# A Mamba block between two feed-forward layers: output blocks copied out of PSUM by ScalarE and added up by GpSimd, and rings of seven for x and the gate

## The reference

```
proj = x @ in_proj                      # gate (4096), x (4096), B and C (128 each), dt (64 heads)
x, B, C = silu(conv4(x, B, C) + bias)   # causal, 4 taps, per channel
dt = softplus(dt + dt_bias);  cum = cumsum(dt * A) in chunks
scores = (C B^T) * exp(cum_i - cum_j) * dt_j        # masked, in a chunk
y = scores @ x + exp(cum) * (C @ state) + D * x     # state: scan over chunks
h = y * silu(gate)
out = (h * rsqrt(mean(h^2)) * norm_w) @ out_proj    # 4096 -> 256
```

## Time and profile before

| | |
|---|---|
| median of 3 runs | 1473.42 us |
| the profiled execution | 1473.38 us, its span 1471.7 us |
| TensorE (PE) busy | 1333.7 us, 91% |
| VectorE (DVE) busy | 1191.9 us, 81% |
| ScalarE (ACT) busy | 1007.0 us, 68% |
| GpSimd (POOL) busy | 820.3 us, 56% |

### The profile page before, as it was taken

The page is one execution under the profiler, slowest core; times in us unless marked ns, Lnnn a source line. Parts: engine busy times, 40 slices in busy tenths (PEclk is TensorE's granted clock), DMA queues, the critical chain, the costliest instruction groups (busy, mean ns, idle before and its releaser), DMA issues. The chain is left out here.

```text
span 1471.7 us, 27111 instructions
## 1 busy us (share of the span) xinstructions
PE 1333.7 (91%) x8896; PEld 1134.4 (77%) x8896; DVE 1191.9 (81%) x2643; ACT 1007.0 (68%) x2067; POOL 820.3 (56%) x896
## 2 busy tenths in 40 slices
PE   5889887767999999999999999999999999986998
PEld 4778766556888878888888888888888888864887
DVE  5753433676999999999999999999999999986433
ACT  1114433667889988888988898888899888861332
POOL 1004211004678777878877787797787878681000
PEclk9999998988999999999999999999999999996999
DMA  6221000222444444453444444444444444334000
GB/s 128 66 86 36 15 6 10 58 65 73 125 111 98 126 117 109 119 115 98 119 128 108 117 105 116 116 122 117 112 104 120 123 110 116 94 80 185 15 14 29
DMA packets 102085, 136.43 MB, mean 93 GB/s; under 512 B 27744, under 2 KB 49856, under 8 KB 101824
## 3 DMA queue, kind: packets, MB, share of 16 engines
q1 hardware_dynamic: 99840, 132.67, 34.4%
q10 hardware_dynamic: 2112, 2.10, 0.4%
HBM read 124.76 MB, written 9.96 MB: 92 GB/s over the span
## 5 line engine op out<-in xcount | busy, mean ns | idle before, releaser
L845 ACT ACTIVATE M<-cum_row,cum_table 128x128 f32<-128x128 f32 x1024 | 312.1, 390 | 0.0
L1272 DVE SCALAR_TENSOR_TENSOR xs<-psum,conv_w_sb,xs 128x509 f32<-128x509 f32 (+2 forms) x384 | 283.2, 738 | 0.4
L985 POOL TENSOR_TENSOR hid_lo<-hid,hid_hi 128x512 fp32r<-128x512 f32 x128 | 196.2, 1533 | 67.3 <-PE psum L40 61.5
L1060 POOL TENSOR_TENSOR hid<-hid,sg 128x512 f32<-128x512 f32 x128 | 165.5, 1293 | 94.0 <-DVE hid L1340 93.9
L1049 POOL TENSOR_TENSOR squares<-squares,sq 128x512 f32<-128x512 f32 x124 | 160.0, 1290 | 75.3 <-ACT sq L822 75.3
L1299 DVE TENSOR_TENSOR M<-M,CB 128x1024 f32<-128x1024 f32 x128 | 183.5, 1434 | 0.0
L1655 PE MATMUL psum<-M,xdt 128*64 128x128 f32 x2048 | 140.1, 278 | 24.3 <-DVE psum L1331 24.2
L827 ACT ACTIVATE sg<-psum 128x512 f32<-128x512 f32 x128 | 75.1, 587 | 104.5 <-PE psum L40 96.9
L1655 PEld LDWEIGHTS psum<-M,xdt 128*64 128x64 f32 x2048 | 110.1, 136 | 47.2 <-DVE M L1299 27.4
L1632 PE MATMUL psum<-xend,B_tok 128*128 128x128 f32 x1024 | 140.1, 281 | 2.5 <-DVE carry L1323 2.4
L853 ACT ACTIVATE M<-M 128x1024 f32<-128x1024 f32 x128 | 134.5, 1051 | 0.5
(11 more groups left out here) (210 smaller groups left out, 3422.0 us busy)
## 6 DMA issues: line engine op xcount, KB each, us to landing
cum_row<-cum_scratch SPq DMA_DIRECT2D x256, 256.0 KB, 4.4
e_row<-e_scratch SPq DMA_DIRECT2D x256, 128.0 KB, 3.4
xw_raw<-L_attn_in_proj_w_dram SPq DMA_DIRECT2D x32, 128.0 KB, 3.3
wo_raw<-L_attn_out_proj_w_dram SPq DMA_DIRECT2D x32, 128.0 KB, 3.0
gw_raw<-L_attn_in_proj_w_dram SPq DMA_DIRECT2D x16, 256.0 KB, 4.5
x_res<-_attn_hidden_states_dram ACTq DMA_DIRECT2D x4, 512.0 KB, 9.4
x_scratch<-x_res SPq DMA_DIRECT2D x4, 512.0 KB, 2.6
x_res<-x_scratch SPq DMA_DIRECT2D x1, 2048.0 KB, 8.0
```

The source lines that it names most:

```text
L845: last = nc.scalar.activation(M[:, v % 3, h, c * CH:(c + 1) * CH], cum_row[:, v % 2, h, c * CH:(c + 1) * CH], ACT.Relu, bias=scalar_of(CUM ...
L985: nc.gpsimd.tensor_tensor(hid_lo[:], hid[:, v % 2, :], hid_hi[:, v % 2, :].bitcast(F32), ALU.subtract).then_inc(hid_lo_done, 1)
L1060: nc.gpsimd.tensor_tensor(hid[:, v % 2, :], hid[:, v % 2, :], sg[:, v % 8, :], ALU.mult).then_inc(hid_done, 1)
L1272: nc.vector.scalar_tensor_tensor(xs[:, v % 8, shift:], psum[:, X_BANK + v % 2, 0:TT - shift], tap_of(v, step), xs[:, v % 8, shift:], ALU.m ...
```

## The change

VectorE's `add_out` goes. In its place ScalarE copies both banks to a new tile `part` (two halves, one buffer) with `take_out`, right behind `square(s)` of the next phase round; GpSimd adds the halves to `mixed` with `add_part`, one in the third and one in the fourth round of the next group of four, behind `split_hid`. In the first group of pairs ScalarE copies straight into `mixed`. `out_proj` now waits for the copies (`out_taken`), and `take_out` waits until `part` has been added up (`mixed_done`). The rings `xs` and `sg` lose one place each, so that `evac_g(v)` waits for `gate(v-7)` and `evac_x(v)` for `skip_path(v-7)`. Second definitions of two helpers, and an unused one, are deleted too; they change no instruction.

```
-    xs = sb("xs", [P, 8, TT], F32)
-    sg = sb("sg", [P, 8, TT], F32)
+    xs = sb("xs", [P, 7, TT], F32)
+    sg = sb("sg", [P, 7, TT], F32)
...
+    part = sb("part", [P, KT, TT], F32)
...
             def evac_g(v):
                 act.wait_ge(g_proj, nth(v))
-                act.wait_ge(hid_done, nth(v - 8))
+                act.wait_ge(hid_done, nth(v - 7))
...
             def evac_x(v):
                 act.wait_ge(x_proj, nth(v))
-                act.wait_ge(v_done, nth(v - 8))
+                act.wait_ge(v_done, nth(v - 7))
...
+            def take_out(v):
+                t = at_slot(v)[1]
+                act.wait_ge(out_done, nth(v))
+                if v == GP - 1:
+                    act.wait_ge(cum_out, 16 * 2 * NT)
+                if v >= SLOTS:
+                    act.wait_ge(mixed_done, KT * ((v - SLOTS) // GP))
+                for m in range(KT):
+                    to = mixed[:, m, tile(t)] if v < SLOTS else part[:, m, :]
+                    nc.scalar.activation(to, psum[:, OUT_BANK + m, :], ACT.Copy).then_inc(out_taken, 1)
...
             for s in range(-8, ALL):
                 if alive(s):
                     square(s)
+                if s > 0 and s % GP == 0:
+                    take_out(s - 1)
                 phase = s % GP == 0 and alive(s + 4)
...
+            take_out(ALL - 1)
...
+            def add_part(v, m):
+                t = at_slot(v)[1]
+                pool.wait_ge(out_taken, KT * (v // GP) + m + 1)
+                nc.gpsimd.tensor_tensor(mixed[:, m, tile(t)], mixed[:, m, tile(t)], part[:, m, :],
+                                        ALU.add).then_inc(mixed_done, 1)
...
                     gate(s + 1)
                     split_hid(s + 1)
                 g, u = divmod(s, SLOTS)
+                if s % GP in (2, 3) and SLOTS <= s - s % GP - 1:
+                    add_part(s - s % GP - 1, s % GP - 2)
...
+            for m in range(KT):
+                add_part(ALL - 1, m)
...
-                if s >= 0 and s % GP == GP - 1:
-                    add_out(s)
...
                 if j == 0:
-                    pe.wait_ge(mixed_done, KT * (v // GP))
+                    pe.wait_ge(out_taken, KT * (v // GP))
```

More of the change, by code:

```diff
@@ L470, in macaron @@
     halo_in, halo_step, halo_done = sem("halo_in"), sem("halo_step"), sem("halo_done")
-    folded = sem("folded")
+    folded, out_taken = sem("folded"), sem("out_taken")
     wo_hi_done, wo_lo_done, hid_hi_done, hid_lo_done = [sem(n) for n in ("wo_hi_done", "wo_lo_done", "hid_hi_done", "hid_lo_done")]
@@ L1009, in split_wo @@
                 split_wo_lo(p)
[L1011 to L1034, removed]
-                                        ALU.subtract).then_inc(wo_lo_done, 1)
-            def hid_to_lo(v):
-                pool.wait_ge(hid_hi_done, nth(v))
-                pool.wait_ge(sq_done, nth(v))
-                nc.gpsimd.tensor_tensor(hid_lo[:, v % 2, :], hid[:, v % 2, :], hid_hi[:, v % 2, :].bitcast(F32),
-                                        ALU.subtract).then_inc(hid_lo_done, 1)
             def add_squares(v):
@@ L1339, in skip_path @@
                 p = pair_of(v)
-                nc.vector.scalar_tensor_tensor(hid[:, v % 2, :], xs[:, v % 8, :], d_sb[:, p:p + 1], bank(Y_BANK),
+                nc.vector.scalar_tensor_tensor(hid[:, v % 2, :], xs[:, v % 7, :], d_sb[:, p:p + 1], bank(Y_BANK),
                                                ALU.mult, ALU.add).then_inc(v_done, 1)
-            def add_out(v):
-                j, t = at_slot(v)
-                dve.wait_ge(out_done, nth(v))
-                if v == GP - 1:
-                    dve.wait_ge(cum_out, 16 * 2 * NT)
-                for m in range(KT):
-                    if v < SLOTS:
-                        nc.vector.tensor_copy(mixed[:, m, tile(t)], psum[:, OUT_BANK + m, :]).then_inc(mixed_done, 1)
-                    else:
-                        nc.vector.tensor_tensor(mixed[:, m, tile(t)], psum[:, OUT_BANK + m, :], mixed[:, m, tile(t)],
-                                                ALU.add).then_inc(mixed_done, 1)
             dve.wait_ge(lut_in, 16)
@@ L1620, in turn_x @@
                 for c in range(CPT):
-                    last = nc.tensor.transpose(psum[:, XT_BANK, c * P:(c + 1) * P], xs[:, v % 8, c * CH:(c + 1) * CH], ident[:])
+                    last = nc.tensor.transpose(psum[:, XT_BANK, c * P:(c + 1) * P], xs[:, v % 7, c * CH:(c + 1) * CH], ident[:])
                 last.then_inc(x_turned, 1)
```

16 lines of the change are left out of this document (8 added, 8 removed).

## The result

The changed kernel takes 1606.99 us (median of 4 runs, 1606.28 to 1611.78) against 1473.57 (4 runs on the same chip): ratio 1.0913, 95% interval 1.0885 to 1.094, or +133.4 us. The forecast was 1583, a loss of 110. The profiled span is 1604.6 us against 1471.7; TensorE is busy 1379.7 us of it (86%, before 91%) at a mean granted clock of 0.938 (0.969).

What follows compares the result with a forecast made beforehand. It took the path from ScalarE's phase round through `e_row` and `scale_off` to TensorE's `diag` to have no slack. 1473.4 + 88.6 (copies, wait, end) + 21 (clock) = 1583 us; range 1495 to 1640, the forecast's own 1540 to 1630.

Steps and rivals of the forecast that it cites:

- the wait for `part`: From round 24 on, ScalarE's copies wait 2.2 us for GpSimd's second add; with copies, 82.6 us over 25 stretches.
- the loop: Copies, ScalarE's phase work, `e_row`, `diag`, two TensorE rounds, `hid_lo`, add, next copies: 33.3 to 35.2 us per four rounds.
- VectorE's adds go: VectorE loses 32 pairs of 1.28 us, 41 us in all; nothing gained on the path, since `e_row` ends there too.
- copies on ScalarE: Two PSUM copies, 1.20 us, ahead of each phase round's table load; 4 us in rounds 4 to 20, without waiting.
- adds on GpSimd: 72 us of adds have room beside GpSimd's 161 of 200; later `hid_lo` costs 0 to 8 us, taken as 0.
- ring of seven, under the wait: `evac_g` 1.1 us later behind its round's gate, hidden by the copies' wait (up to 2.2 us): 0; uncovered 27 us.
- What would show it: ScalarE idle 2 us before copies, some 25 waits for `e_row`, TensorE idle 3 us, stretches 33 to 37 us.
- two rounds of TensorE, `hid_lo`: Way from `diag(71)` to `hid_lo` of 72, which starts when `out_proj` ends: 13.20 us from s = 68.
- as the one from u = 4 ... so I take 3.4 for it too: Stretch from u = 8, with the weight load behind `e_row`: +3.4 us, as from s = 68.
- rival 4: VectorE's adds were the true limit, `e_row` early enough: 35 us less, 2 more at the end, 1440 us; chance 0.05.
- The clock: TensorE's idle time halves its clock for one block, 1.27 us, in two of three of 25 stretches: 21 us.
- Rival 2: Every TensorE stall halves the clock for two blocks' worth, 64 us: 1626 us; chance 0.09.

Runs made afterwards that it cites:

- the ReLUs first: The changed kernel with ScalarE's ReLUs of slot s+3 moved ahead of the copies and SiLUs in a phase round: 1552.1 us.
- filling the stall: The changed kernel with eight more 512-column matmuls on TensorE ahead of `diag(s+1)` in each stretch's second round, from round 17 on: 1602.6 us.

## Why the prediction was right, and where it was off

The time fell into the range, and the wait for `part` came where it was forecast. The way in which the loop closes was right in part only, and some of the agreement is luck.

The parts, added one after the other (1472, 1459.8, 1489.4, 1513.6, 1595.8, 1607.0), beside the terms of the sum. In another order the shares would differ: the ring costs 11 us under the wait and 51 alone.

| part | forecast us | measured us |
|---|---|---|
| VectorE's adds go | 0 | -12 |
| copies on ScalarE | with the wait: 82.6 + 4 + clock 21 | 30 |
| adds on GpSimd | 0 (0 to 8) | 24 |
| wait for `part` | (see copies) | 82 |
| ring of seven, under the wait | 0 | 11 |
| end | 2 | 4 (the tail; in the lines above) |
| sum | 110 | 135 |

- *What would show it* came as written: 17 waits of ScalarE ahead of the copies in 600 us (up to 2.0), 16 of `scale_off` for `e_row`, TensorE idle for up to 3.5 us ahead of `diag`, a clock below 1.00. On average only the stretches from u = 8, at 38.2 us, are above the 33 to 37.
- *The loop's size* came out nearly: copies and wait cost 112 us with the clock in it, forecast 108. ScalarE waited 2.03 us where 2.2 was forecast. The stretches from u = 4 and u = 12 took 35.5 and 34.3 us, forecast 35.2 and 34.1 without the clock. Measured as the sum was made, from copies to copies, the loops from u = 0, 4, 8 and 12 took 35.2, 36.1, 37.2 and 35.8 us (means of the same four groups), forecast 33.3, 35.2, 35.8 and 34.1: all four are 0.9 to 1.9 us longer, and the forecast's 21 us for the clock are 0.8 in each of 25.
- *The loop's way* was right up to `diag` and wrong behind it, and its terms were off in opposite ways, which is luck. From the copies of s = 68 to the next ones: copies 1.11 (forecast 1.20), to `load_cum` 9.08 (9.08), to `scale_off(71)` 6.80 (7.85), to `diag(71)` 0.85 (0.84), to `hid_lo` of 72 15.10 (13.20), `hid_lo` and the add 2.54 with 0.09 to the copies (2.99), in all 35.57 (35.2). The step that failed here is "two rounds of TensorE, `hid_lo`", with "`hid_lo` has one buffer and follows `out_proj` in every row". From u = 0 and u = 8 `hid_lo` ahead of the second add did wait for `out_proj` (0.7 to 1.2 us, in 12 of 13 loops). But in 11 of the 12 loops from u = 4 and u = 12 it began 1.2 to 2.3 us behind the end of `out_proj`, held up by GpSimd's own list. TensorE comes into these a round earlier: `hid_lo` ahead of the first add waited for it 0.6 to 2.4 us in 10 of the 11. Only by so much is the forecast's way longer than the second loop, which the prediction didn't add up.
- *`e_row`* is what TensorE's `diag` waits for, as forecast, by way of `scale_off` (47.1 us, and 43.3 of `scale_off` for `e_row`). That this wait alone makes the kernel slower isn't shown: the ReLUs first took it away and 55 us with it, but shortened the second loop by some 2.4 us or more at the same time, in each of the 25.
- *The stretches from u = 0 and u = 8* were mis-sized: 36.3 and 38.2 us, forecast 33.3 and +3.4 (35.8). The step that failed there is "The adds on GpSimd ... have room beside its 161 of 200". That is an average over 200 us; in rounds u = 14 to 0 GpSimd had 21.98 of 23.19 us. The adds cost 15 us in the stretches from u = 0 and 20 in the whole loop, not 0 to 8. From u = 8 it is at least in part the gate weights, whose split came late: moving it a round earlier took 3.6 us off the stretch (with the ReLUs first). The prediction had put this case aside, with "as the one from u = 4 ... so I take 3.4 for it too".
- *The ring*: "that cover hides up to 2.2 us" held for the most part, 11 us under the wait. Uncovered it costs 51, not 27; the prediction counted phase rounds alone.
- *VectorE's relief*: 12 us, between "they bring nothing" and the 35 of rival 4.
- *The clock*: from round 16 on it was at half for about 102 us (3.4 before). What that cost isn't settled. In the changed kernel the stretches from u = 4 with a spell at half clock took 35.8 us on average (four), the two without 34.5: 1.25 us, as the forecast's 1.27. With the rings of seven alone, those from u = 8 took 35.2 with and 33.7 without. But filling the stall removed 18 of 30 spells and gave 4 us, or some 16 with the fill's own price added, an estimate. So the clock's part lies between those 4 us and some 37 (30 such spells at 1.25); the forecast of 21 lies between them and isn't shown.

Rival 2 let each stall halve the clock, by the rule of the Trainium skill in "TensorE: Matmul & The Clock Gate", section "HAM oscillation — how this bites in real kernels". The trace agrees only in part. Behind the 3.22 us of idle time ahead of `diag(71)` the clock stayed at 1.00, behind 2.91 ahead of `diag(75)` (at 990.04) it was at 0.50, its level of 1.2 GHz, for most of the next 7 us (columns as above):

```profile
955.00:962.00 7.00, 7.00 (x51) 6.07 (x50) 7.00 (x17) 6.35 (x15) 6.23 (x7) 1.00 0.61 128
990.00:997.00 7.00, 5.58 (x26) 4.34 (x27) 6.26 (x14) 4.65 (x12) 6.86 (x6) 0.54 0.82 135
```

## What to carry to other kernels

A copy out of PSUM that frees one engine can cost most on the engine that does it: ask what stands behind it in that engine's list, above all what other engines' loads wait for, and put that first. A buffer of one place between a fast and a late engine closes a loop; add up its length by rows, and do it for every way round: here a second loop, past TensorE, was nearly as long as the one that was added up. A sum that comes out within a few per cent doesn't show that its way is the right one; compare it term by term. Read an engine's room in the rounds in which the new work falls, not from a mean: here the mean said 39 of 200 us and the rounds had 1.2 of 23.

## What was not expected of the hardware

The length of an idle time alone doesn't tell what the clock does: 3.22 us were harmless where 2.91 were not. And GpSimd's instructions of two inputs and 512 columns last longer where VectorE's multiply of 1024 columns (L1294) has begun before them and still runs: 1.94 us (median of 45 rows of 500 to 1300 us) instead of 1.28 (236 rows that don't overlap it). Where the GpSimd row began first, it kept its length (1.30, 30 rows). One such place, in round 69 of the changed kernel, VectorE first:

```profile
949.83 1.22 DVE L1294 TENSOR_TENSOR M<-M,CB 128x1024 f32<-128x1024 f32 x1
```

```profile
950.14 2.04 POOL L1033 TENSOR_TENSOR squares<-squares,sq 128x512 f32<-128x512 f32 x1 [6.45 <-ACT sq L823]
```

The GpSimd row starts 0.31 us behind the VectorE row, and what is left of that one, 0.91 us, is about what it lasts longer than 1.28 (0.76). The Trainium skill says in "SBUF — State Buffer", section "SBUF: two separate sides", that of two such instructions the one that starts second waits for the whole of the first; the rows agree to some 0.2 us.
